# An uneven table for the maxima's units, and other slots for the V product, its copy and the first statistics

## What is computed

```python
mod = (silu(c) @ wmod).reshape(8, 6, 1, 128)            # sa, ca, ga, sb, cb, gb
h = layernorm(x) * (1 + ca) + sa
q, k, v = split(h @ qkv_w.T + qkv_b)                     # rotary embedding on q and k
attn = softmax(where(causal, q @ k.T / sqrt(8), -1e9))   # per batch and head
x = x + ga * ((attn @ v) @ proj_w.T + proj_b)
h = layernorm(x) * (1 + cb) + sb
y = square(relu(h @ W_fc.T)) @ W_proj.T                  # 512 hidden features
x = x + gb * (number of spikes of y in 5 leaky steps) / 5
```

## Time and profile before

| | us |
|---|---|
| median of 3 runs | 450.79 |
| lowest and highest | 449.61, 452.21 |
| the profiled execution | 447.9 |
| its span, first to last instruction | 446.1 |
| setup before the first exponential | 49.2 |
| batches 0 to 7, from the first exponential of each | 43.7, 45.9, 48.0, 49.1, 48.2, 47.9, 45.6, 43.7 |
| after the last exponential | 24.8 |

### The profile page before, as it was taken

One profiled execution on the slowest core, in us unless ns is written; L12 is line 12 of the kernel. 1 busy time (PEld: TensorE's weight loads), 2 busy tenths in 40 slices (PEclk: granted clock), 3 DMA queues, 4 the chain that ended last, 5 costly groups with the idle time before them and its releaser, 6 DMA issues.

```text
span 446.1 us, 15629 instructions
## 1 busy us (share of the span) xinstructions
PE 389.0 (87%) x6603; PEld 251.9 (56%) x6603; DVE 320.0 (72%) x718; ACT 263.3 (59%) x459; POOL 125.4 (28%) x163
## 2 busy tenths in 40 slices
PE   3878989878999999998999989999999889888883
PEld 3326655545656665666557655666566646654653
DVE  6659987857884999478965998489956875631275
ACT  7203556576677666765686657766676558467522
POOL 7714211421341052403250244205340320040120
PEclk9989999999999999999999999999999999999999
DMA  6056463242424332232414241323224040011000
GB/s 212 24 159 168 110 203 107 67 128 70 113 60 114 77 101 79 92 95 49 137 62 133 54 135 60 110 62 96 79 82 106 25 137 17 16 38 28 3 24 25
DMA packets 26049, 38.53 MB, mean 86 GB/s; under 512 B 5796, under 2 KB 20716, under 8 KB 23692
## 3 DMA queue, kind: packets, MB, share of 16 engines
q1 hardware_dynamic: 25980, 37.53, 29.3%
HBM read 26.35 MB, written 8.65 MB: 78 GB/s over the span
## 4 chain that ended last, share of the span: by engine, by line
PE 42%; DVE 18%; DMA 12%; issue 9%; ACT 8%; SPq 6%; POOL 5%; ACTq 0%; POOLq 0%; DVEq 0%
PE o_bank L606 9%; PE d_bank L523 8%; PE t_bank L588 6%; DVE negmax L955 6%; PE s_bank L543 5%; DMA kf<-k_scr 3%; SPq L440 3%; ACT probs L809 3%; DVE xn L971 3%; PE a_bank L523 2%; DMA rden<-r_scr 2%; DMA r_scr<-rden_c 2%; DMA den<-o_raw 2%; PE t_bank L523 2%; SPq L444 2%
## 5 line engine op out<-in xcount | busy, mean ns | idle before, releaser
L955 DVE TENSOR_REDUCE negmax<-s_bank 128x1 f32<-128x512 f32 (+7 forms) x368 | 192.2, 565 | 66.3 <-PE s_bank L549 65.0
L809 ACT ACTIVATE probs<-t_bank 128x512 f32<-128x512 f32 x288 | 163.5, 595 | 87.5 <-PE t_bank L593 83.1
L543 PE MATMUL s_bank<-kf,qf 126*64 126x512 bf16 (+7 forms) x1024 | 118.5, 292 | 18.3 <-DVE negmax L955 15.4
L588 PE MATMUL t_bank<-qf,kf 128*64 128x512 bf16 (+7 forms) x1024 | 112.0, 288 | 10.2 <-ACT probs L809 8.9
L543 PEld LDWEIGHTS s_bank<-kf,qf 126*64 126x64 bf16 x1024 | 49.5, 109 | 50.4 <-DVE negmax L955 36.2
L606 PE MATMUL o_bank<-probs,v 128*32 128x512 f32 (+7 forms) x1024 | 75.2, 412 | 0.0
L549 PE MATMUL s_bank<-causal,identb 128*64 128x64 bf16 x1024 | 72.0, 194 | 0.0
L593 PE MATMUL t_bank<-causal_t,identb 128*64 128x64 bf16 x1024 | 64.4, 195 | 0.0
L588 PEld LDWEIGHTS t_bank<-qf,kf 128*64 128x64 bf16 x1024 | 41.2, 110 | 31.6 <-ACT probs L809 11.5
L593 PEld LDWEIGHTS t_bank<-causal_t,identb 128*64 128x64 bf16 x1024 | 47.6, 110 | 9.2
L549 PEld LDWEIGHTS s_bank<-causal,identb 128*64 128x64 bf16 x1024 | 46.6, 111 | 8.3 <-issue 8.2
(11 more groups left out here) (144 smaller groups left out, 441.6 us busy)
## 6 DMA issues: line engine op xcount, KB each, us to landing
qf<-q_scr SPq DMA_DIRECT2D x15, 576.0 KB
kf<-k_scr SPq DMA_DIRECT2D x45, 192.0 KB
q_scr<-parts SPq DMA_DIRECT2D x24, 128.0 KB, 1.7
k_scr<-parts SPq DMA_DIRECT2D x24, 128.0 KB, 1.7
xa<-in_x SPq DMA_DIRECT2D x8, 256.0 KB, 3.8
o_t<-o_raw SPq DMA_DIRECT2D x60, 32.0 KB, 2.2
rden<-r_scr SPq DMA_DIRECT2D x15, 128.0 KB
out_y<-count SPq DMA_DIRECT2D x7, 256.0 KB, 7.2
```

The lines of the kernel that those rows point to most:

```text
L543: nc.tensor.matmul(bank[C * a:C * (a + 1), col:col + keys], qf[0:KS, slot, 2 * p + a, C * i:C * (i + 1)], kf[0:KS, slot, 2 * p + a, 0:keys ...
L588: nc.tensor.matmul(bank[C * a:C * (a + 1), col:col + w], kf[0:KX, slot, 2 * p + a, C * kb:C * (kb + 1)], qf[0:KX, slot, 2 * p + a, C * kb: ...
L809: nc.scalar.activation(probs[:, v, :], t_bank[u % 2][:, :], ACT.Exp, scale=SCALE).then_inc(e_done, 1)
L955: last = nc.vector.tensor_reduce(own[:, i, p:p + len(same)], cols, AX.X, ALU.max, negate=True)
```

## The change

A table `S_PACE` gives the units of each slot of a batch: two in slots 0, 1, 27, 29, 32 and 34, one in all others, 42 per batch as before. `scores_ahead` sums it instead of the even pace; the lead of 31 and batch 0's limit stay. TensorE and VectorE both take their units from it. Within a half the units then fall as follows (batch-wide slots 24 to 35):

| slot | 24 | 25 | 26 | 27 | 28 | 29 | 30 | 31 | 32 | 33 | 34 | 35 |
|---|---|---|---|---|---|---|---|---|---|---|---|---|
| before | 17, 18 | 19 | 20 | 0 | 1 | 2 | 3, 4 | 5 | 6 | 7 | 8 | 9 |
| after | 15 | 16 | 17 | 18, 19 | 20 | 0, 1 | 2 | 3 | 4, 5 | 6 | 7, 8 | 9 |

The V product moves from slot 0 to slot 5 on TensorE and its copy from slot 1 to slot 6 on ScalarE. `statistics1` moves from slot 13 to slot 0 and `normalise1` from slot 17 to slot 3 on VectorE, and `deviation1` on GpSimd moves ahead of the maxima split and of `normalise_outputs`.

```diff
+S_PACE = [2, 2, 1, 1, 1, 1] + [1] * 21 + [2, 1, 2, 1] + [1, 2, 1, 2, 1]
+S_DONE = [sum(S_PACE[:at + 1]) for at in range(PER_BATCH)]
...
-A_AT = {-16: T1, -13: QK, -9: QK + 1, 0: V_}
+A_AT = {-16: T1, -13: QK, -9: QK + 1, 5: V_}
...
 def scores_ahead(u):
-    return min(NS * HALVES, -(-(u + 1) * NS // NU) + S_LEAD, S_START + S_RISE * (u + 1))
+    b, at = divmod(u, PER_BATCH)
+    return min(NS * HALVES, 2 * NS * b + S_DONE[at] + S_LEAD, S_START + S_RISE * (u + 1))
...
-                if at == 1 and 0 < b < final:
+                if at == 6 and 0 < b < final:
                     place_values(b + 1)
...
-                    if at - PER_BATCH == -23:
+                    if at == 0:
                         statistics1(b + 2)
-                    if at - PER_BATCH == -19:
+                    if at == 3:
                         normalise1(b + 2)
...
             for b in range(NB):
+                if b + 2 < NB:
+                    deviation1(b + 2)
                 split_maxima(2 * b + 1)
                 pool.wait_ge(rows_loaded, 16)
                 if b > 0:
                     normalise_outputs(b - 1)
-                if b + 2 < NB:
-                    deviation1(b + 2)
```

## The result

The changed kernel takes 469.36 us (median of 4, 466.66 to 472.82) beside 451.50 us for the kernel before on the same chip: ratio 1.040, 95% interval 1.035 to 1.045. The direction was as forecast; the time lies 9.5 us above 459.9 and 3.9 above the range's upper end of 465.5. The profiled execution took 466.66 us (span 464.8), 18.8 more than that of before. Medians take in every execution; ratios and intervals leave out those more than 1.5% above the fastest of the same kernel.

The account below looks back on a forecast made before the run. TensorE's own order of work was taken to bound the kernel. Batches 2 to 5 +4.0, batch 1 +1.9, batch 0 +3.0, batch 6 +1.7, batch 7 -1.5 gave +9.1: 450.8 + 9.1 = 459.9 us, range 453 to 466 (448.5 to 465.5 with the even case).

Parts of the forecast that it names:

- What bounds it: Whole loop: TensorE's own order of work bounds it, busy 44.80 of 48.25 us per full batch, 3.4 us of gaps.
- The unit in slot 27: Slot 27's second unit waits for a reduce behind slot 25's reciprocals, late behind the spread: TensorE stall near 3 us.
- The outputs earlier: Head of the batch: V's move makes the outputs' copy about 0.9 us earlier and the projection 1.1 us earlier.
- Slot 28 0.4 later: Start of slot 28: 1.63 us later from the stall, less 1.2 from earlier reciprocals, so 0.4 us later.
- The split: GpSimd's maxima split behind unit 20 delays slot 29's cast to 3.15 us after slot 28: 0.8 us more per batch.
- Batch 0: Early statistics and normalisation on VectorE add 2.3 us, partly hidden; reciprocals start 0.6 later; the batch loses 3.0 us.
- Batch 7's gain: Slot 8's unit no longer waits 1.56 us behind slot 6's reciprocals, its needed unit now in slot 5: -1.5 us.
- Gaps close: Rival: spread traffic does not hold the denominators, reciprocals run about 265.3 in batch 4; -6.5, 444.3 us; chance 0.17.
- on an idle queue: Last batch, no spread traffic: reciprocals ran 3.8 us after the copy feeding the denominators' DMAs; evidence for the faster rival.
- the sum: All batches: 4.0 + 1.9 + 3.0 + 1.7 - 1.5 = +9.1 us against the profiled execution.
- upper bound of +15: Highest case: output chain gains nothing, reciprocals stay where they are; 1.2 us more in each of five batches.

Follow-up runs that it names:

- e2: The changed kernel with slot 25's reciprocals moved behind the units of slot 27 on VectorE: 443.25 us (ratio 0.987 to the kernel before).
- e13: The changed kernel with the first half's denominator DMAs issued ahead of the spread for half 2b+3, not behind it: 464.52 us (ratio 1.031).
- e9: The changed kernel with reciprocals behind slot 27's units and maxima split behind GpSimd's first rest, plus unused maxima on VectorE ahead of slot 25's unit: 473.69 us.
- e10: As e9, plus nine pairs of unused products on TensorE inside slot 27's wait: 460.83 us (ratio 1.023).
- e12: Kernel before, even pace, with V and statistics moves (not batch 0's statistics), slot 25's reciprocals behind slot 27's units, maxima split behind first rest: 441.04 us.
- e1: The changed kernel with three pairs of unused products on TensorE ahead of slot 27's last unit: 462.30 us (ratio 1.029).

## Why the prediction was right in direction and wrong in size

Each low stretch's price is read from the same work at both levels. From the start of slot 27's second unit to the next batch's first exponential it is 16.49 us in batches 3 and 4 at full clock, 18.03 in batch 2 and 18.13 in batch 5. In batch 0 it is 15.97, in batch 6 15.49, beside 14.50 and 13.87 in e2 at full clock. In batch 1, from the end of the keys' wait to the transposes of slot 13, it is 7.40, beside 5.77 in e2. Batch 7 takes 43.66, beside 42.05 in e2 and e13. The last column is the forecast's term:

| batch | change | of it the clock | rest | forecast |
|---|---|---|---|---|
| 0 | +4.1 | 1.48 | 2.7 | +3.0 |
| 1 | +4.0 | 1.62 | 2.4 | +1.9 |
| 2 | +3.1 | 1.54 | 1.5 | +1.0 |
| 3 | -0.5 | 0 | -0.5 | +1.0 |
| 4 | +1.9 | 0 | 1.9 | +1.0 |
| 5 | +2.7 | 1.64 | 1.0 | +1.0 |
| 6 | +3.5 | 1.62 | 1.9 | +1.7 |
| 7 | 0.0 | 1.61 | -1.7 | -1.5 |
| sum | 18.7 | 9.5 | 9.2 | +9.1 |

- *What bounds it* held: TensorE's order bounds the loop, and its gaps grew from 3.4 us in batch 4 to 5.85 (50.16 - 44.31).
- *The unit in slot 27* held, on its own mechanism: a wait "near 3 us" was 1.6 to 3.8, with reciprocals before the reduce and a wait for den before those. Issue of the spread to reciprocals was 9.9 to 11.0 us where 11.0 was taken; they started at 30.9 to 32.5 us of batches 2 to 5, forecast 31.7. e13 shows the step on which it rested.
- *The outputs earlier* held on average: in batches 2 to 5 the copy is 0.9 us earlier (forecast 0.9), the projection 0.2 to 1.9, on average 0.9 (1.1). In batch 4, from whose rows the 1.1 was worked out, it is 0.2.
- *Slot 28 0.4 later*: first hidden product on average 0.3 later over batches 2 to 5, less the clock.
- *The split* held: the cast stands 3.13 us behind slot 28 (3.15), the rest of the batch takes 0.8 longer, and the wait for relu is above 1 us.
- *Batch 0*: the term's own figures (2.3, less 1.15, less 0.75) give reciprocals 0.4 us later, not the 0.6 that it takes, and they start at 30.7 us of the batch in both kernels. That its 3.0 came near the 2.7 measured is luck.
- *Batch 7's gain* was there, 1.6 us, and was covered by a low stretch of the same size. At e2's clock it shows: 42.05 us.
- *"Gaps close"* fell, twice over. Its condition didn't hold, and e13 shows that its price was too good where it does: VectorE reaches the reciprocals at 30.1 us of batches 2, 3 and 5, not 29.4, and 0.99 us of wait are left. The 3.8 us "on an idle queue" that it leans on hold 2.65 us in which SyncE issues the four DMAs one after another (402.25 to 404.90 in batch 7 of before); the last lands at most 1.1 us after that.
- **The step that failed is the sum**: it took each wait at its own length and had no term for the clock at which TensorE works after it. That term measured 9.5 us, 1.5 to 1.6 for each of six stretches, and it is the whole miss: 18.7 less 9.1 is 9.6. (20.5 us at the lower level times the 0.41 of e9 and e10 would give 8.4; with the time inside waits left out, both come to 0.47 or 0.48 us for each.) That the rest sums to 9.2 beside 9.1 is partly luck, since single batches are off by up to 1.5 us (batch 3) either way. The same holds for the range: its upper bound of +15 was drawn from the same terms, so it could not contain the clock's. The trace of before held the warning in a form I passed over: two low stretches outside the batches, in setup and at the end, where TensorE also waits.

The Trainium skill says so in words: "TensorE: Matmul & The Clock Gate", section "What's actually happening", has the clock set by how busy TensorE has lately been. The traces agree: what was idle in e9 and filled with unused products in e10 decided it.

## What to carry to other kernels

A new wait on a nearly saturated TensorE can cost more than its length: here each stretch at the lower clock cost another 1.5 to 1.6 us, so a sum of waits wants a second term, and its range an upper end that has a low stretch behind every one. When a second unit of work is put in one slot, look at who frees its buffer, and at what stands ahead of that on the other engine: a short step with a late input (the reciprocals) belongs behind the work that someone waits for. Test a placement by moving the suspected step before giving up the table; with two steps moved, the same table went from 4% slower to over 2% faster. Then test the kernel without the table too: the even pace did as well (e12).

## What the runs showed that I had not expected

Adding products whose results nobody uses to the engine that bounds the kernel made it 7 us faster (e1) and 13 us faster (e10 against e9). The kernel had the helper for it all along: its setup and its end call `keep_warm`, its loop does not. And the same wait need not have the same result: in e13 the wait of 2.38 us for the keys at 182.57 is followed by the full clock and that of 2.36 us at 232.39 by the lower one.

```profile
182.50:185.90 3.40, 3.33 (x52) 1.99 (x56) 2.72 (x5) 2.26 (x5) 0.56 (x1) 1.00 0.07 20
232.90:236.30 3.40, 3.40 (x30) 1.71 (x28) 2.47 (x4) 2.22 (x4) 0.86 (x1) 0.50 0.19 61
```

In the changed kernel a wait of 2.52 us (batch 4) had none and one of 2.18 (batch 5) had one. In slot 27, the waits of 2.95 us and more in e9 all had one, those of 1.43 and less in e10 none. What decides between these lengths stays open, and so does how many of the changed kernel's waits draw one in a given execution: its four runs had mean clocks of 0.958 to 0.972, and spread over 6 us. The kernel before may draw some as well: its mean clocks in the runs beside the experiments are 0.979 to 0.998, where its profiled execution has 0.994 and none in the batches.
